# A DLRM tower on one NeuronCore: the third group's second stage two slots sooner, and another last sum over d

## The reference

```
e = stack of table rows                          # 1024 x 32 x 16 (d is the last axis)
xk = e
for W in (W0, W1, W2):                           # W0 32x32x64, W1 and W2 32x64x64
    xk = relu(einsum('bmd,bhd,mhk->bkd', e, xk, W))
    outs.append(sum(xk, axis=2))                 # over d
z = concatenate(outs, axis=1)                    # 1024 x 192
h = concatenate([z, dense_ctx], axis=1)          # 1024 x 208
h = relu(h @ W_top1 + b_top1)                    # 512 wide
h = relu(h @ W_top2 + b_top2)                    # 256 wide
y = h @ W_top3
```

## Time and profile before

| | us |
|---|---|
| median of 3 runs | 644.87 (644.58 to 645.04) |
| the profiled execution | 644.13 |
| its span, first to last instruction | 642.3 |
| TensorE busy | 584.2 |
| VectorE busy | 584.5 |
| ScalarE busy | 358.1 |
| GpSimd busy | 469.8 |
| granted clock of TensorE, mean | 1.000 of full speed |

### The profile page before, as it was taken

The page is one execution under the profiler, slowest core; times in us unless marked ns, Lnnn a source line. Parts: engine busy times, 40 slices in busy tenths (PEclk is TensorE's granted clock), DMA queues, the critical chain, the costliest instruction groups (busy, mean ns, idle before and its releaser), DMA issues.

```text
span 642.3 us, 7779 instructions
## 1 busy us (share of the span) xinstructions
PE 584.2 (91%) x2896; PEld 209.1 (33%) x2896; DVE 584.5 (91%) x329; ACT 358.1 (56%) x594; POOL 469.8 (73%) x405
## 2 busy tenths in 40 slices
PE   0078999999998989999999999999999999999998
PEld 0023333232322323333334323333334323333455
DVE  1039899999999999999999999999999999999994
ACT  0006474657556465747676465747576565736552
POOL 6677769798888888888979788888979793803011
PEclk9999999999999999999999999999999999999999
DMA  5286596637181825547280826456370916300000
GB/s 162 46 320 155 220 289 166 264 65 298 35 284 50 259 106 153 212 80 285 53 310 5 278 85 195 170 119 245 64 300 15 299 53 202 160 3 2 1 2 1
DMA packets 27138, 96.51 MB, mean 150 GB/s; under 512 B 7414, under 2 KB 12540, under 8 KB 22876
## 3 DMA queue, kind: packets, MB, share of 16 engines
q1 hardware_dynamic: 18908, 93.90, 43.5%
q0 software_dynamic: 8192, 2.11, 2.7%
HBM read 80.25 MB, written 15.73 MB: 149 GB/s over the span
## 4 chain that ended last, share of the span: by engine, by line
DVE 42%; PE 27%; issue 12%; POOL 10%; DMA 5%; SPq 1%; ACT 1%; DVEq 0%; POOLq 0%; ACTq 0%
DVE prod L489 41%; PE acca L590 10%; PE accb L590 8%; POOL emb L362 7%; DMA rows<-field_dram 3%; PE acc L560 3%; POOL prod L380 3%; PE spread L633 2%; DMA field_dram<-zb_field 1%; PE accb L611 1%; PE acc L611 1%; SPq L280 1%; DVE prod L470 1%; DVE za L494 0%; ACT zb_field L720 0%
## 5 line engine op out<-in xcount | busy, mean ns | idle before, releaser
L362 POOL DMA_INDIRECT emb<-in_table,idx x256 | 247.2, 966 | 77.8 <-issue 67.6
L590 PE MATMUL acca<-prod,w 128*64 128x512 f32 x1024 | 229.1, 594 | 3.3 <-DVE prod L489 2.1
L590 PE MATMUL accb<-prod,w 128*64 128x512 f32 x960 | 216.4, 596 | 13.3 <-DVE prod L489 13.3
L380 POOL TENSOR_TENSOR prod<-rows,mates 128x1024 f32<-128x1024 f32 x70 | 164.4, 2380 | 16.0 <-issue 15.6
L489 DVE TENSOR_TENSOR prod<-rows,x1a 128x2048 f32<-128x2048 f32 x64 | 145.6, 2278 | 5.2 <-ACT x1a L725 2.5
L489 DVE TENSOR_TENSOR prod<-rows,x1b 128x2048 f32<-128x2048 f32 (+1 forms) x65 | 145.7, 2245 | 1.3 <-PE accb L590 0.7
L489 DVE TENSOR_TENSOR prod<-rows,x2a 128x2048 f32<-128x2048 f32 x64 | 145.7, 2277 | 1.1 <-PE accb L590 0.8
L489 DVE TENSOR_TENSOR prod<-rows,x2b 128x2048 f32<-128x2048 f32 x64 | 145.6, 2277 | 0.0
L590 PEld LDWEIGHTS acca<-prod,w 128*64 128x64 f32 x1024 | 71.7, 137 | 145.8 <-issue 136.1
L590 PEld LDWEIGHTS accb<-prod,w 128*64 128x64 f32 x960 | 65.6, 137 | 155.7 <-issue 113.7
L725 ACT ACTIVATE x1a<-acc 64x512 f32<-64x512 f32 x62 | 35.3, 570 | 124.5 <-PE acc L560 123.8
(11 more groups left out here) (74 smaller groups left out, 256.4 us busy)
## 6 DMA issues: line engine op xcount, KB each, us to landing
rows<-field_dram SPq DMA_DIRECT2D x30, 2048.0 KB, 13.6
field_dram<-zb_field SPq DMA_DIRECT2D x32, 256.0 KB
mates<-field_dram SPq DMA_DIRECT2D x16, 512.0 KB, 3.8
emb<-in_table,idx POOLq DMA_INDIRECT x256
field_dram<-zb_field SPq DMA_DIRECT2D x32, 128.0 KB
field_dram<-zb_field SPq DMA_DIRECT2D x16, 192.0 KB
rows<-field_dram SPq DMA_DIRECT2D x2, 1024.0 KB, 7.0
rows<-field_dram SPq DMA_DIRECT2D x1, 1536.0 KB, 12.6
```

The source lines that it names most:

```text
L362: pool.indirect_dma_start(out=emb[q % EMBS][:, j * EMB:(j + 1) * EMB], out_offset=None, in_=table, in_offset=bass.IndirectOffsetOnAxis(ap= ...
L380: nc.gpsimd.tensor_tensor(prod0[:, (q * L0 + k) % RING0, :], rows[:, slot(q, t), :], mates[:, :], ALU.mult).then_inc(s_prod0p, 1)
L590: mm = nc.tensor.matmul(acc[j % 2][side * HID:(side + 1) * HID, :], (w1 if layer == 1 else w2)[:, step, :], prod[:, (made(layer, s, half, ...
```

## The change

Two edits.

The first is in the table of places: stage 1 of group 2 (the second half of its first dense layer) moves from behind the first block of slot 29 to behind the last block of slot 27, and stage 2 (its second dense layer) from behind the third block of slot 29 to behind the first. ScalarE evicts the moved stage at the start of slot 28, between x2a and x1a.

The second is in the last sum over d. GpSimd first adds the eight values of d of stream 30 to four (64x256, written d by d into a free part of zin12). VectorE then takes the two parts of stream 31 out of PSUM, one after the other, each with one instruction that relus it and adds it to these four values, adds four values to two, and two to one, which goes to zb. VectorE's relu and its reduction over 16 values go, and so does ScalarE's relu of stream 31.

```diff
-                (27, 1): (2, 0), (29, 0): (2, 1), (29, 2): (2, 2), (30, 0): (2, 3),
+                (27, 1): (2, 0), (27, 3): (2, 1), (29, 0): (2, 2), (30, 0): (2, 3),
...
+        last_sums = zin12[0][0:HID, :]
...
@@ gpsimd, behind halve3(LAST - 1)
+            pool.wait_ge(s_z3, SUBS - 1)
+            pool.wait_ge(s_za, PERIODS - 1)
+            first = zin3[third(LAST), :].rearrange("k (b d) -> k d b", d=EMB)
+            nc.gpsimd.tensor_tensor(last_sums[:, 0:PART].rearrange("k (d b) -> k d b", b=BT), first[:, 0:QUAD, :],
+                                    first[:, QUAD:DH, :], ALU.add).then_inc(s_last_four, 1)
...
@@ vector, sum3(LAST)
-                    s, by_d = 2 * p + 1, zin3[third(p), :].rearrange("k (b d) -> k d b", d=EMB)
+                    s = 2 * p + 1
                     dve.wait_ge(s_used, taken(2, s, 1, UNITS - 1))
-                    nc.vector.tensor_scalar_max(by_d[:, DH:DH + DH // 2, :],
-                                                sums_alone(s)[0:HID, 0:PART].rearrange("k (d b) -> k d b", b=BT),
-                                                0.0).then_inc(s_z3v, 1)
-                    dve.wait_ge(s_z3, 2 * p + 2)
-                    dve.wait_ge(s_z3v, 1)
-                    sum_d(zb[0:HID, p * BT:(p + 1) * BT], zin3[third(p), :], EMB, s_zb)
+                    dve.wait_ge(s_last_four, 1)
+                    for c in range(2):
+                        wait_for(dve, s_last_add, c)
+                        nc.vector.scalar_tensor_tensor(last_sums[:, 0:PART], sums_alone(s)[c * HID:(c + 1) * HID, 0:PART], 0.0,
+                                                       last_sums[:, 0:PART], ALU.max, ALU.add).then_inc(s_last_add, 1)
+                    dve.wait_ge(s_last_add, 2)
+                    nc.vector.tensor_tensor(last_sums[:, 0:2 * BT], last_sums[:, 0:2 * BT], last_sums[:, 2 * BT:PART],
+                                            ALU.add).then_inc(s_last_add, 1)
+                    dve.wait_ge(s_last_add, 3)
+                    nc.vector.tensor_tensor(zb[0:HID, p * BT:(p + 1) * BT], last_sums[:, 0:BT], last_sums[:, BT:2 * BT],
+                                            ALU.add).then_inc(s_zb, 1)
...
@@ scalar
-                    for c in range(2) if s < SUBS - 1 else (1,):
+                    for c in range(2):
...
+                if (j - 1, 3) in TOWER_AT:
+                    tower_step(*TOWER_AT[j - 1, 3])
                 if j < SUBS - 2:
                     input1(j + 2, 0)
-                for i in range(4 * UNITS):
+                for i in range(3):
...
-            z3(SUBS - 1)
```

More of the change, by code:

```diff
@@ L230, in cin_tower_kernel @@
         s_tower, s_act, s_y = sem("s_tower"), sem("s_act"), sem("s_y")
-        s_wide, s_ones, s_z3v = sem("s_wide"), sem("s_ones"), sem("s_z3v")
+        s_wide, s_ones = sem("s_wide"), sem("s_ones")
+        s_last_four, s_last_add = sem("s_last_four"), sem("s_last_add")
         s_last1, s_last_h1, s_last2 = sem("s_last1"), sem("s_last_h1"), sem("s_last2")
```

## The result

| | median us | runs | lowest to highest |
|---|---|---|---|
| kernel before | 644.79 | 13 | 644.35 to 645.93 |
| changed kernel | 643.61 | 13 | 642.90 to 645.53 |

The ratio of the changed kernel to the one before is 0.9983, with a 95% interval from 0.9975 to 0.9992. That is 1.1 us, between 0.5 and 1.6. The forecast was 643.8, 1.07 us sooner. The interval excludes 1, so the changed kernel is faster; whether by more than 0.2% it leaves open.

A forecast was written before the change was run, and what follows sets the result against it. TensorE was taken to bound slots 28 to 31, VectorE's products the slots before, two VectorE instructions the tail. Gains 0.81 + 0.26 = 1.07 took 644.13 to 643.06; 0.74 up to the median gave 643.8 us, range 643.2 to 644.7.

The forecast's parts named there:

- TensorE's own sum: Slots 28 and 29: slot 28 is 1.27 us later, slot 29 saves 2.08, net -0.81 from slot 30 on.
- 0.09 to spare: First block of slot 30: due at 600.49, its product there at 600.40, so TensorE would not wait.
- rival (a): VectorE sets the pace in slot 30, late products eat about half of 0.81: 644.2 us, chance 0.10.
- What VectorE makes of it: Slots 28 and 29: new waits of 0.13, 0.75, 0.53; two old waits go, 0.64; last product 0.77 us later.
- the cover: ScalarE's eviction of the moved stage stays hidden, as the top-2 stage needs h1 only at 586.4; no cost.
- The tail: Last block's end to the next matmul on zb_field: 1.73 us instead of 1.99, 0.26 less.
- Rival (b): In the tail the two relu-and-adds cost 596 ns each: tail +0.08, 644.1 us, chance 0.14.
- The cap of 0.30: Tail's gain is at most about 0.30 us, TensorE's idle before 636.23; its bias and top-1 matmuls lie under that.
- The rule against the tail: Many small VectorE tiles each pay a fixed part; the objection was put at 0.51 us for two more steps.
- (c): The moved stage's new place gives nothing, the 0.59 of idle returns elsewhere, only the tail counts: 644.6 us, chance 0.05.
- (d): Slower: the bound goes over to VectorE at the pair two behind slot 29's top-2 stage: 646.2 us, chance 0.03.
- Rival (e): More than worked out, through a tail at its cap and better luck in slot 30: 643.5 us, chance 0.06.

The follow-up runs named there:

- The fourth experiment: Changed kernel with stage 1 of group 2 behind the last block of slot 28 instead of slot 27: 645.52 us, ratio 1.0011 to the kernel before.
- the strided version: Changed kernel with the last sum's four values per sample side by side, stride 16 words, instead of d by d in a row: tail 2.02 us, one execution.
- the first experiment: Kernel before with only the move of stages 1 and 2 and ScalarE's eviction, last sum as before: 644.18 us, ratio 0.9993 to the kernel before.

## Why the prediction was right

**What bounds it: right.** TensorE from slot 28 on, VectorE before, as its reading of the earlier trace rows had it. Stage 1 at a place without idle gave nothing, at a place with idle its idle and restart, twice.

**TensorE's own sum: -0.81, measured -0.70.** Up to slot 30 it holds: slot 28's first block ends 568.85 - 563.33 = 5.52 behind slot 27, before 567.09 - 562.85 = 4.24, so 1.28 later where 1.27 was forecast. Slot 30 is due at 600.97 - 563.33 = 37.64 against 38.45: 0.81 sooner, to the hundredth. Then the first block takes 3.57 in place of 3.43. The step that failed is the margin: "0.09 to spare" was counted as no cost. Its product was there at 598.56 + 2.28 + 0.05 = 600.89, 0.08 before TensorE came, and the block still paid a restart of 0.14. With 0.8 us or more to spare no block did. (Of the 0.14, 0.02 comes back in the last four blocks, 6.91 in place of 6.93.) The second margin, worked out at 0.07, was 0.22 and cost nothing: that block comes behind the y stage and takes 3.58, as before. So rival (a), that VectorE takes something back in slot 30, came true with 0.14 of the 0.4 that I gave it, and through the restart, not through a wait.

**What VectorE makes of it: right.** Three waits, by the starts of the products 0.12, 0.84 and 0.43 where 0.13, 0.75 and 0.53 were worked out, the two old ones gone, the last product 0.76 later where 0.77 was forecast.

**ScalarE: right for this kernel, and the cover was real.** Its eviction ran from 567.33 to 568.17 and x1a behind it still waited 8.5 us. The fourth experiment shows what a missing cover costs: 0.98 us when stage 2 follows at once.

**The tail: -0.26, measured -0.28, by a sum with two errors that hide each other.** The relu-and-adds took 422 ns (425 taken), the additions 283 and 216 (289 and 222). But the steps between them cost 0.03, not 0.10: the term of the earlier trace rows belonged to an instruction with two waits. VectorE was thus ready at 1.50 and not at 1.68, and the tail stopped at 1.71 because TensorE's own matmuls of za and bias end there. The cap of 0.30 that the earlier trace rows showed was the true bound, the sum of VectorE's steps was not. That 1.73 came within 0.02 of the measured 1.71 is luck: the 0.18 too much in VectorE's steps happens to be about what TensorE's queue adds behind them (1.50 to 1.71). Rival (b), 596 ns each, fell; the strided version shows it is the layout that avoided it. In the chain the first matmul on zb_field also takes 0.42 in place of 0.49: it overlaps the bias matmul in front of it by 0.07, where before it stood behind an idle. That was not in the sum. So the profiled executions differ by 0.70 + 0.28 + 0.07 = 1.05 from zero to the end, forecast 1.07.

**From the piece to the whole time.** The sum was 1.07 and the medians are 1.18 apart, with an interval of 0.5 to 1.6 by the ratio, so the medians can't tell 1.07 from its neighbours; it is the pieces that bear the sum out. The forecast for the profiled execution, 643.06, was 0.55 too low, because the execution that it started from, 644.13, was an early one: it lies below all 13 timings of the kernel before, and 0.49 of the difference stands before the zero. The step by 0.74 up to the median took that out again.

**The rule against the tail.** The fixed part per instruction (the Trainium skill, VectorE: DVE Perf Modes, TRN2 errata) stands in these rows: the additions from SBUF take 216 ns for 64 elements and 283 for 128, which leaves some 150 ns that don't depend on the count. The estimate of 1.10 us for the four, worked out from that page's cycles, was short; they took 422 + 422 + 283 + 216 = 1.34. Four small steps still beat two large ones, because they go over 576 elements fewer (704 against 1280) and write in a row.

**GpSimd: hidden, but 1.09 in place of 0.72.**

```profile
628.49 1.09 POOL L446 TENSOR_TENSOR zin<-zin 64x256 f32<-64x256 f32 x1 [0.15 <-ACT zin L751]
```

It ended at 629.58, 4.5 us before VectorE asked. Its inner loop steps by 16 words where the halving of the same count steps by one; strided output or not it took the same (1.11), so it would be the reads, which wasn't tried alone.

**The chances.** (c) fell with the first experiment, (d) with the last product 0.76 later. Rival (e) took idle and restart for all there is to win. That holds for this change, but 0.71 more lay beside it, in moving stage 0 too.

## What to carry to other kernels

When two engines feed each other through a ring of buffers, a move is worth the idle that it fills in front of the gapless stretch, and only if the engine that it holds up gets its time back: work out both engines, pair by pair, and test half of the move, since here half of it lost 0.58 where all of it won 0.68. A margin under a tenth of a microsecond was not a margin here: the block paid most of a restart though its product was there. In a chain of small dependent steps count the semaphores in front of each one, keep the intermediate values in a row, and then check what the next engine still has in its own queue, because that becomes the bound.

## What the runs showed of the hardware

- A block of eight matmuls behind another takes 3.43 us if its product has been there for 0.8 us or longer, and 3.57 if it was there for 0.08 or 0.09 us; behind an idle it takes 3.65.
- A second, long satisfied semaphore in front of a VectorE instruction costs 0.06 to 0.07 us (gaps of 0.10 against 0.03 and 0.04).
- 64x256 words out of PSUM, relued and added, take 422 ns written in a row and 605 ns with a stride of 16 words in the second input and the output.
- GpSimd's addition of 64x256 took 1.09 us with an inner step of 16 words in its reads, against 0.72 for the halving of the same count.
